# One loop of sixteen steps for both halves of heads in the second layer's self attention

## What is computed

```python
# L1 self attention, N_HEAD = 16, D_K = D_V = 64, on the normalised x
q = (z @ wq) @ fcq_w + fcq_b      # wq: 512 -> 64, fcq_w: 64 -> 16 * 64
k = (z @ wk) @ fck_w + fck_b
v = (z @ wv) @ fcv_w + fcv_b
# per head and sequence of 32 tokens
attn = softmax(q k^T / 8)
x = x + concat_heads(attn v) @ fco_w + fco_b
```

## Time and profile before

| | us |
|---|---|
| median of 3 executions | 2039.45 |
| lowest, highest | 2036.78, 2045.35 |
| the profiled execution, its time | 2039.55 |
| its span | 2037.7 |
| PE busy | 1751.1 (86%) |
| DVE busy | 896.6 (44%) |
| POOL busy | 816.6 (40%) |
| ACT busy | 602.4 (30%) |

### The profile page before, as it was taken

One profiled execution on the slowest core, in us unless ns is written; L12 is line 12 of the kernel. 1 busy time (PEld: TensorE's weight loads), 2 busy tenths in 40 slices (PEclk: granted clock), 3 DMA queues, 4 the chain that ended last, 5 costly groups with the idle time before them and its releaser, 6 DMA issues. The chain is left out here.

```text
span 2037.7 us, 38262 instructions
## 1 busy us (share of the span) xinstructions
PE 1751.1 (86%) x13882; PEld 1408.1 (69%) x13882; DVE 896.6 (44%) x1782; ACT 602.4 (30%) x1213; POOL 816.6 (40%) x542
## 2 busy tenths in 40 slices
PE   5785999883899997899999999968783598999999
PEld 4443777662687786788888888756562486878877
DVE  4545262447567844133333322345565433333332
ACT  3112151441233334233333343335353211111111
POOL 1001332104548985232333333222103099793922
PEclk8996999986899998999999999977896799999999
DMA  6692001853557796111111111010333455452534
GB/s 219 218 345 84 25 1 63 311 210 152 212 177 230 252 228 184 32 32 43 31 31 32 40 31 32 11 47 7 138 128 145 181 169 183 148 181 87 180 68 98
DMA packets 108938, 254.08 MB, mean 125 GB/s; under 512 B 9712, under 2 KB 26736, under 8 KB 108816
## 3 DMA queue, kind: packets, MB, share of 16 engines
q1 hardware_dynamic: 77472, 189.86, 27.3%
q0 software_dynamic: 10752, 25.34, 5.4%
q10 hardware_dynamic: 20592, 37.22, 5.4%
HBM read 182.24 MB, written 70.13 MB: 124 GB/s over the span
## 5 line engine op out<-in xcount | busy, mean ns | idle before, releaser
L140 PE MATMUL banks<-ra_DE 128*128 128x258 f32 (+2 forms) x912 | 318.4, 350 | 30.2 <-ACT fa_DE L2144 8.5
L141 PE MATMUL banks<-ra_DE 128*128 128x258 f32 (+2 forms) x912 | 308.3, 339 | 0.0
L142 PE MATMUL banks<-ra_DE 128*128 128x258 f32 (+2 forms) x912 | 307.7, 338 | 0.0
L140 PE MATMUL banks<-weights_F,rest_r_F 128*128 x552 | 229.6, 416 | 15.8 <-ACTq L1662 13.3
L140 PEld LDWEIGHTS banks<-ra_DE 128*128 128x128 f32 (+1 forms) x912 | 175.8, 193 | 62.6 <-ACT fa_DE L2144 14.8
L141 PE MATMUL banks<-weights_F,rest_r_F 128*128 x552 | 218.4, 396 | 0.0
L142 PE MATMUL banks<-weights_F,rest_r_F 128*128 x552 | 218.3, 395 | 0.0
L142 PEld LDWEIGHTS banks<-ra_DE 128*128 128x128 f32 (+1 forms) x912 | 176.1, 193 | 18.7
L141 PEld LDWEIGHTS banks<-ra_DE 128*128 128x128 f32 (+1 forms) x912 | 176.6, 194 | 15.7
L1609 POOL TENSOR_TENSOR weights_F<-rest_F,weights_F 128x1536 fp32r<-128x1536 f32 x52 | 182.1, 3502 | 4.2
L2111 POOL TENSOR_TENSOR fa_DE<-fa_DE 128x1028 f32<-128x1028 f32 x32 | 60.9, 1902 | 254.4 <-DVE fa_DE L2207 254.4
(11 more groups left out here) (482 smaller groups left out, 3504.7 us busy)
## 6 DMA issues: line engine op xcount, KB each, us to landing
rest_F<-in_L_units SPq DMA_DIRECT2D x52, 768.0 KB, 4.2
rest_C<-in_L_units SPq DMA_DIRECT2D x28, 768.0 KB, 4.8
fa_DE<-in_ctxT SPq DMA_DIRECT2D x32, 514.0 KB, 4.0
e_sorted<-zeros_AB SPq DMA_DIRECT2D x1, 12220.0 KB, 36.8
rest_C<-e_sorted ACTq DMA_DIRECT2D x47, 260.0 KB, 5.0
e_y_scratch<-zeros_AB SPq DMA_DIRECT2D x1, 12032.0 KB, 67.7
e_y_scratch<-rest_C ACTq DMA_DIRECT2D x47, 256.0 KB, 4.8
tail_F<-in_L_units SPq DMA_DIRECT2D x12, 768.0 KB, 18.2
```

Of the source, the lines that this page charges most:

```text
L140: pe.matmul(psum, lh, rh, start=first, stop=False)
L141: pe.matmul(psum, lh, rl, start=False, stop=False)
L142: return pe.matmul(psum, ll, rh, start=False, stop=last)
```

## The change

- Both halves' weights are one set of loads (`both_weights`): SP issues `fcqk`, `fcv` and `fco_w` of both halves, two of each, ahead of the constants in the block of the low-rank product.
- One product block (`both_halves`) makes the q and k codes of both halves: 32 jobs, eight PSUM banks, even jobs evicted by DVE and odd ones by ACT. The codes of heads 8 to 15 go to two new buffers `qt1` and `kt1`, which take the memory of `xh` and `xl` (closed just before).
- One loop of sixteen steps: step s works on tokens tile s // 2 and half s % 2, so that the set `u` is the half. The order within a step is as before.
- The bias is added to x at even steps, the row statistics are taken at odd ones. The add of an odd step waits for that of the even one.
- The zero fill is issued at the start of the one loop.

The diff, cut to its core:

```diff
-            first_half = half_weights(tag, low_rank, 0, HD, EC, f1, r1, rqk, rv)
+            if low_rank:
+                both = both_weights(tag, HD, EC, f1, r1)
+                programs = both[1]
+            else:
+                first_half = half_weights(tag, low_rank, 0, HD, EC, f1, r1, rqk, rv)
...
                 @block.sync
                 def _(eng):
-                    first_half[1][0](eng)
+                    programs[0](eng)
                     constant_loads(eng)
...
+            if low_rank:
+                both_halves(tag, scale, HD, EC, bo, pb, bqc, bkc, rqk, rv, turned_codes(), *both)
+                return
...
+        def both_weights(tag, HD, EC, f1, r1):
...
+            weights = ([(*wqk[hh], d["L1_attn_fcqk"][:, half[hh]]) for hh in range(2)]
+                       + [(*wv[hh], d["L1_attn_fcv"][:, half[hh]]) for hh in range(2)]
+                       + [(*wo[hh], d["L1_attn_fco_w"][half[hh], :].rearrange("(c p) n -> p c n", p=P)) for hh in range(2)])
...
+        def both_halves(tag, scale, HD, EC, bo, pb, bqc, bkc, rqk, rv, q1k1, buffers, programs):
...
+            qt, kt = [q0k0[0], q1k1[0][:]], [q0k0[1], q1k1[1][:]]
+            jobs = [(hh, k, e, h) for hh in range(2) for k in range(2) for e in range(EC) for h in range(NHALF)]
+            NB = 8
...
+                @block.gpsimd
+                def _(eng):
+                    programs[2](eng, (2, 3, 4, 5))
+
+                @block.scalar
+                def _(eng):
+                    for j, (hh, k, e, h) in enumerate(jobs):
+                        if j % 2:
+                            eng.wait_ge(s_mm, j + 1)
+                            act.activation(dst_of(hh, k, e, h), banks[:, j % NB, :], ACT.Identity,
+                                           bias=bias_of(hh, k, e)).then_inc(s_out_a, 1)
+                        if j in (0, 2, 4, 10):
+                            programs[1](eng, ((0, 2, 4, 10).index(j) + 2,))
+
+                @block.vector
+                def _(eng):
+                    for j, (hh, k, e, h) in enumerate(jobs):
+                        if j % 2 == 0:
+                            eng.wait_ge(s_mm, j + 1)
+                            dve.tensor_scalar(dst_of(hh, k, e, h), banks[:, j % NB, :], bias_of(hh, k, e), None,
+                                              ALU.add).then_inc(s_out_v, 1)
+
+                @block.tensor
+                def _(eng):
+                    for j, (hh, k, e, h) in enumerate(jobs):
+                        if j >= NB:
+                            eng.wait_ge((s_out_v, s_out_a)[j % 2], (j - NB) // 2 + 1)
+                        cols, tok = slice(e * P, (e + 1) * P), slice(h * HALF, (h + 1) * HALF)
+                        rows = slice(DH * k, DH * k + DH)
+                        eng.wait_ge(s_w[hh], 1)
+                        mm3(banks[:, j % NB, :], wqk[hh][0][rows, cols], wqk[hh][1][rows, cols],
+                            rqk[0][rows, tok], rqk[1][rows, tok]).then_inc(s_mm, 1)
...
+            STEPS_ALL = 2 * NT
+            def all_steps(engine, step, before=lambda i: None, after=lambda: None):
+                with engine.Fori(0, NT - 2) as i:
+                    before(i)
+                    for u in range(2):
+                        step(i, 2 * i + u, u)
+                    after()
+                for s in range(STEPS_ALL - 4, STEPS_ALL):
+                    step(s // 2, s, s % 2)
...
+                    def add(n, s, u):
+                        eng.wait_ge(s_y, s + 1)
+                        if u == 0:
+                            eng.wait_ge(s_xb, n + 1)
+                        else:
+                            eng.wait_ge(s_xa, s + LEAD)
+                        dve.tensor_tensor(x[:, n, :], banks[:, 4 * u, :], x[:, n, :], ALU.add).then_inc(s_xa, 1)
+                        if u:
+                            row_statistics(eng, s_xa, s + 1 + LEAD, s_passed, n)
```

More of the change, by code:

```diff
@@ L780, in _, with self_attention @@
                         values(NT - 1, 1)
-        def self_attention(tag, low_rank):
+        def self_attention(tag, low_rank, turned_codes=None):
             scale = float(DH) ** -0.5
@@ L849, in _ @@
                 def _(eng):
-                    first_half[1][2](eng, (0, 1))
+                    programs[2](eng, (0, 1))
                     constants(eng)
@@ L860, in _ @@
                         if j == 0:
-                            first_half[1][1](eng, (0, 1))
+                            programs[1](eng, (0, 1))
                 @block.vector
@@ L1231, in step @@
                         output(n, u)
+                    scores(0, 0)
+                    scores(1, 1)
+                    values(0, 0)
+                    all_steps(pe, step)
+        def both_weights(tag, HD, EC, f1, r1):
+            f, r = Area(fa, F_SIZE, f1), Area(ra, R_SIZE, r1)
+            q0k0 = f.take(EC, T), f.take(EC, T)
+            f2 = f.at
+            tail = Area(fa, F_SIZE, F_SIZE - 4 * HD).take(4, HD)
+            staging = [tail[:, k, :] for k in range(4)] + [f.take(EC, D) for _ in range(2)]
+            half = [slice(hh * HD, (hh + 1) * HD) for hh in range(2)]
+            r_ot = r.at
+            wqk, wv = ([(r.take(HD), r.take(HD)) for _ in range(2)] for _ in range(2))
+            wo0 = r.take(EC, D), r.take(EC, D)
+            xg = [(r.take(P), r.take(P)) for _ in range(2)]
+            wo1 = r.take(EC, D), r.take(EC, D)
+            wo = wo0, wo1
+            weights = ([(*wqk[hh], d["L1_attn_fcqk"][:, half[hh]]) for hh in range(2)]
+                       + [(*wv[hh], d["L1_attn_fcv"][:, half[hh]]) for hh in range(2)]
+                       + [(*wo[hh], d["L1_attn_fco_w"][half[hh], :].rearrange("(c p) n -> p c n", p=P)) for hh in range(2)])
+            return (q0k0, f2, r_ot, xg, (wqk, wv, wo)), split_programs(f"{tag}w", weights, staging)
@@ L2389, in build @@
                 else:
-                    xh, xl = (area(name, [P, DC, T], F32R) for name in ("xh", "xl"))
+                    if part == "AB":
+                        xh, xl = (area(name, [P, DC, T], F32R) for name in ("xh", "xl"))
                     fa, na, zeros = area("fa", [P, F_SIZE]), area("na", [P, N_SIZE]), area("zeros", [P, D + 8])
@@ L2399, in build, with second_codes @@
                     else:
+                        normed = stack.enter_context(ExitStack())
+                        xh, xl = (normed.enter_context(nc.sbuf_tensor(f"{name}_{part}", [P, DC, T], F32R))
+                                  for name in ("xh", "xl"))
+                        def second_codes():
+                            normed.close()
+                            return [area(name, [P, DC, T]) for name in ("qt1", "kt1")]
                         cross_heads()
-                        self_attention("sb", True)
+                        self_attention("sb", True, second_codes)
                     free_semaphores()
```

163 lines of the change are left out of this document (added).

## The result

The changed kernel takes 2029.76 us (median of 13 executions, 2026.85 to 2034.56), the kernel before 2040.89 in the same comparison; the ratio is 0.9945, 95% interval 0.9934 to 0.9957. That is 11.2 us faster (8.8 to 13.5), where 7.5 was forecast. One of the 13 executions of the kernel before took 3978.07 us and stays out of the ratio. The time lies inside the stated range of 2021 to 2039.

A forecast was written before the change was run, and what follows sets the result against it. The products were taken as bound by PE at its granted clock, the loops by a ring of ACT and DVE. Terms −11.6 − 5.25 + 8.5 + 0.9 = −7.5 took 2039.55 to 2032.0 us, range 2021 to 2039.

The forecast's parts named there:

- The new product's clock: In the one product of both halves: clock 0.50 throughout, 37.1 us in place of 18.4 + 10.25, +8.5 us.
- Rival A: In the new product: the clock comes back within it or never falls, 2022.2 or 2014.7 us; chance 0.12.
- late recovery: In the new product: clock back just after the first 18.4 us, up to 9.8 us less, 2022.2 us.
- the sum's own rule: In the products: jobs side by side at row group passes let 48 matmuls take the room of 45, 96 of 87.
- One loop less: In the loops: one fill, slow first step and run-out less, 106.7 us in place of 118.3, −11.6 us.
- rival B: In the new loop: the clock stays low, each further slow step costs 2.74 us; chance 0.05.
- The second product and its block end: Between the old loops: the product's 10.25 us at full clock lost, block ends of 1.05 + 4.2 saved, −5.25 us.
- Three passes between row groups: In the new product: three passes in place of two, so 96 matmuls take the room of 87.
- The longer load: Ahead of the product: 1536 KB more before the constants delays PE's start, +0.9 us, bounds 0 and +4.7.
- The chance for "faster": For the whole kernel, below the mark of 2029.3 us: 0.19 + 0.12, against 0.65 same and 0.04 slower.
- main case: For the whole kernel: the terms as summed, 2032.0 us, own spread about 2026 to 2037; chance 0.79.

The follow-up runs named there:

- e2: The changed kernel with 12 idle 128-row matmuls filling PE's wait between the low-rank product and the new product; 2009.55 us, ratio 0.9837.
- e1: The changed kernel with its 96 product matmuls taken over all 128 rows in place of 64; 2017.97 us, ratio to before 0.9887.
- e3: The changed kernel with q and k matmuls issued in turn, in pairs from the two row groups; 2004.86 us, ratio 0.9820.
- e4: The changed kernel's loads and one product, but two loops of eight steps behind it, one per half; 2041.69 us, ratio to before 1.0003.
- e7: e6 with idle matmuls also around the loop's fill, 6 ahead of the first scores and 24 behind the first values; 2001.21 us, ratio 0.9811.
- e6: e3 and the 12 idle matmuls of e2 together, on the changed kernel; 2005.26 us, ratio 0.9832.
- e8: The kernel before without any edit, traced a second time; this execution took 2043.56 us.
- e9: The kernel before without any edit, traced a third time; this execution took 2047.92 us.
- e10: The kernel before without any edit, traced a fourth time; this execution took 2047.04 us.

## Why the prediction was right or wrong

- **The new product's clock, right.** Behind the same 2.96 us of waiting the 64-row matmuls ran at 0.50, 36.5 us for 37.1; by the experiments the wait lets the clock fall (e2) and the 64 rows keep it down (e1). Rival A (the clock comes back within the product) did not happen in any of the three traces. Its price for a late recovery, 9.8 us, counts 48 matmuls as done in the first 18.4 us, where the sum's own rule has the room of 45; by that rule it is 9.1. The Trainium skill ("TensorE: Matmul & The Clock Gate", Part 1) has activity release the throttle. These runs agree for 128 rows (e1, back in 2.7 us) and for two row groups at once (e3), and do not for 64 rows in one group at a time.
- **One loop less, right within 1 to 2 us.** −11.6 was forecast; the mean of the traces gives −10.6, and e4 against the changed kernel 9.7 without the wait between its loops. Steps of 5.96 us in the steady part; rival B (more slow steps) did not happen: one step of 9.1 us. That what went before a loop leaves no trace in it, as I had argued against B, holds only roughly: the second loop took 59.3 us behind a product at 1.00 and 57.4 to 58.5 behind one that had fallen.
- **The second product and its block end, mis-sized.** This is the step that failed. "The second product's 10.25 us at full clock are bought back at nearly double", together with "1.05 + 4.2 go, the 2.75 stay", rested on one trace. From its start to the next scores that product takes 20.0 us in three of four traces, not 14.5. In those executions the move costs 5.6 us less than I had summed, in the mean over the four traces 4.2. The rest of the products' row in the table (5.4 us off in all) is the first product, 0.2 us longer in the mean, and the new one with its block end, 1.0 shorter than summed; the loops take 1.0 back, and the whole stretch is 4.4 us off. −7.5 less 4.2 is −11.7, near the measured −11.2; since the interval is 8.8 to 13.5 and the small terms are off by about a microsecond each, the closeness is partly luck. That matmuls of 64 rows keep a clock of 1.00, as e2 expected, is true behind a busy stretch (e2: 19.8 us at 1.00) and was true in only one of four traces of the kernel before behind the loop's run-out, with its two idle pieces.
- **Three passes between row groups, right.** They stand in the trace as three rows with x2.
- **The longer load, true in one case only.** +0.9 was taken; in the changed kernel's three traces the wait of PE ahead of the product stayed at 2.96 us, so the load cost nothing: the low-rank product had lost time at 0.50 and ended after the constants had landed. With a low-rank product at 1.00, as the prediction had it, the constants come last, and PE waited 1.0 us more in e3 and 0.45 in e4. This is a second place where one trace was taken for all.
- **The chance for "faster", too low.** 0.31 against 0.65 for "same", for a result that lies on the border. The main case's own spread was taken from three times of the kernel before; I did not ask what in the profile makes them spread by 8.6 us. The second product's two outcomes, 5 us apart in the stretch, are a part of the answer. They are not all of it: the changed kernel does not have them, its three traced stretches lie within 1.3 us, and those executions still lie 11.3 us apart (2021.75 to 2033.07). What spreads outside this stage was not looked into.

## What to carry to other kernels

When a term of a sum depends on the clock of one stretch in one trace, read a second trace of the same kernel before pricing it: here the same product took 10 us or 17. Idle time of PE ahead of a dense stretch can cost more than itself: three microseconds of waiting cost 8 in one product, and twelve matmuls that compute nothing bought them back. And where two operand sets sit in different row groups, issue their matmuls in turn: at one clock it nearly halved PE's time here, and it also brought the clock back; after that look at the evictions.

## What the runs showed of the hardware

- Matmuls of 64 rows and 512 columns, on high and low parts written as `fp32r`, back to back, ran 36.5 us at a granted clock of 0.50 (1.2 GHz) without its rising, and 19.8 us at 1.00 (2.4 GHz) without its falling (e2). The same with 128 rows was back at 1.00 2.7 us after the start (e1).
- Two such matmuls in the row groups 0 to 63 and 64 to 127 run at the same time at nearly full pace each: 96 in 14.6 us, a wait of 1.2 included, part of it at 0.50 (e3).
- Idle matmuls behind the first values did not delay the fill: the loop's first p-v came 9.1 us after the first scores (1383.4 to 1392.5 in e7), against 9.5 in the changed kernel. The six ahead of the scores put these off by 0.6 us against e6.
- What decides whether the clock falls in the second product of the kernel before stays open. It did in three of four traces with the same program and the same two idle pieces ahead of it (1.42 and 1.05 us). Whether the chip plays a part is not known: e8 ran on one chip, e9 and e10 on another, and that of the first trace is not on record.
